# A transformer kernel on Trainium2: masks taken with the maxima on VectorE, weight scaling moved behind the first split, two row transfers in halves, and new orders of work

## The reference, cut to what matters

```
x = layernorm(x + attention0(x))   # 16 heads of width 8, low-rank q and k, causal mask, softmax
x = layernorm(x + ffn0(x))         # silu(x W1) * (x W2), two 512x512 layers with gelu, then W3; each weight has a scale per output
x = layernorm(x + attention1(x))   # 16 heads of width 8, no mask, softmax
x = layernorm(x + ffn1(x))         # one of 8 LoRA experts per token, relu, W_out
```

## Time and profile before

| what | value |
|---|---|
| median of 3 runs | 1014.37 us (1014.31 to 1017.72) |
| the profiled execution's own time | 1017.38 us |
| its span, from the first instruction's start to the last one's end | 1015.4 us |
| PE, DVE, ACT busy | 929.3, 630.3, 469.4 us |
| PE, DVE instructions | 7520, 1643 |
| granted TensorE clock, mean | 0.973 of full speed |

### The profile page before, as it was taken

How to read it: one execution, slowest core, us unless ns; L and a number is a source line. 1 busy time by engine, 2 the same in 40 slices (tenths; PEclk the granted TensorE clock), 3 DMA queues, 4 the chain that set the end, 5 groups by cost and what they waited for, 6 DMA issues and landing times.

```text
span 1015.4 us, 19231 instructions
## 1 busy us (share of the span) xinstructions
PE 929.3 (92%) x7520; PEld 720.2 (71%) x7520; DVE 630.3 (62%) x1643; ACT 469.4 (46%) x935; POOL 164.6 (16%) x261
## 2 busy tenths in 40 slices
PE   4489998999899899988999999999999999999885
PEld 4265875778677678876776887677787867778644
DVE  5555358655965884494588547858666477655643
ACT  0043144653356553345765246556345547363451
POOL 2013023000200420120132014003101013201001
PEclk9997999999999999998999999999999989999888
DMA  8403114202310340240034014301421102011200
GB/s 293 119 8 101 42 53 141 80 3 65 90 53 19 88 117 2 63 132 16 4 101 116 2 49 123 102 5 36 128 72 40 49 23 66 5 36 39 74 3 10
DMA packets 48392, 65.16 MB, mean 64 GB/s; under 512 B 5520, under 2 KB 42640, under 8 KB 43312
## 3 DMA queue, kind: packets, MB, share of 16 engines
q1 hardware_dynamic: 46240, 58.61, 20.4%
q10 hardware_dynamic: 2064, 5.34, 1.4%
HBM read 48.46 MB, written 14.68 MB: 62 GB/s over the span
## 4 chain that ended last, share of the span: by engine, by line
PE 71%; DVE 16%; DMA 6%; issue 3%; ACT 2%; SPq 1%; POOL 1%; ACTq 0%; POOLq 0%; DVEq 0%
PE ps_g L885 21%; PE ps_g L816 10%; PE ps_s L798 8%; PE ps_s L775 7%; DVE top L613 6%; PE ps_g L934 5%; PE ps_g L867 4%; PE ps_s L759 3%; PE ps_g L915 2%; PE ps_g L734 2%; PE ps_g L916 2%; DMA inter<-in_w 2%; DMA krow<-scratch 1%; PE ps_s L767 1%; DMA qrow<-tsplit 1%
## 5 line engine op out<-in xcount | busy, mean ns | idle before, releaser
L613 DVE TENSOR_REDUCE top<-ps_s 128x2 f32<-128x512 f32 (+1 forms) x448 | 288.9, 682 | 161.1 <-PE ps_s L759 87.3
L500 ACT ACTIVATE prob<-ps_s 128x384 f32<-128x384 f32 (+1 forms) x512 | 243.5, 551 | 103.3 <-PE ps_s L798 79.2
L798 PE MATMUL ps_s<-qrow,krow 75*128 75x256 bf16 (+1 forms) x1024 | 151.2, 268 | 8.2 <-DMA qrow<-tsplit 5.0
L775 PE MATMUL ps_s<-krow,qrow 72*128 72x256 bf16 x768 | 148.0, 282 | 8.0 <-DVE top L613 6.7
L816 PE MATMUL ps_g<-prob,v 128*32 128x256 f32 (+1 forms) x2048 | 128.1, 370 | 7.2 <-POOL prob L454 4.9
L522 ACT ACTIVATE hid<-ps_g 128x512 f32<-128x512 f32 x64 | 38.2, 597 | 185.9 <-PE ps_g L885 185.8
L798 PEld LDWEIGHTS ps_s<-qrow,krow 75*128 75x128 bf16 x1024 | 87.6, 100 | 47.9 <-ACT prob L500 23.6
L885 PE MATMUL ps_g<-glu,wh 128*128 128x256 f32 x512 | 120.2, 389 | 0.3 <-DVE glu L683 0.2
L885 PE MATMUL ps_g<-hid,wh 128*128 128x256 f32 x512 | 116.4, 381 | 0.0
L885 PEld LDWEIGHTS ps_g<-glu,wh 128*128 128x128 f32 x512 | 97.5, 195 | 14.8 <-DVE glu L683 0.9
L775 PEld LDWEIGHTS ps_s<-krow,qrow 72*128 72x128 bf16 x768 | 69.6, 100 | 48.8 <-DVE top L613 28.8
(11 more groups left out here) (92 smaller groups left out, 1133.0 us busy)
## 6 DMA issues: line engine op xcount, KB each, us to landing
qrow<-scratch SPq DMA_DIRECT2D x32, 576.0 KB
krow<-scratch SPq DMA_DIRECT2D x96, 192.0 KB
scratch<-split SPq DMA_DIRECT2D x96, 128.0 KB, 1.8
xt<-in_xt SPq DMA_DIRECT2D x16, 128.0 KB, 4.2
x<-in_x SPq DMA_DIRECT2D x16, 128.0 KB, 6.6
wh<-in_wh ACTq DMA_DIRECT2D x1, 2048.0 KB, 14.9
out<-xout SPq DMA_DIRECT2D x16, 128.0 KB, 3.1
qrow<-tsplit SPq DMA_DIRECT2D x96, 8.0 KB, 1.8
```

The source lines that it names most:

```text
L500: nc.scalar.activation(prob[s][:, j % 2, g, 0:wide], ps_s2[:, (GROUP * j + g) % PSUM2, 0:wide], ACT.Exp, scale=1.0 / float(np.sqrt(np.floa ...
L613: nc.vector.tensor_reduce(out=dst, in_=src, axis=AX, op=ALU.max, negate=True).then_inc(maxed[s], 1)
L775: done = nc.tensor.matmul(at, queries(h, qb), keys(h, 2), start=True, stop=s == A1, skip_group_check=True)
L798: done = nc.tensor.matmul(bank[:, kb * SEQ:(kb + 1) * SEQ - q0], krow[s][n % DEEP[s]][0:ROWSM, h, kb * P:(kb + 1) * P], qrow[s][n % DEEP[s ...
```

## The change

- **Masks.** PE's mask matmuls stay for chunks 0 and 1 of A0 (`BY_PE = 2`). From chunk 2 on PE writes bare scores, and DVE replaces the one reduction of a bank by `tensor_tensor_reduce`: (scores + triangle) * -1, written back to PSUM, with the running minimum as the accumulator output. There are four instructions over 128 elements for u = 0 and two over 256 elements for u = 1 and 2. The tile `above` gets a left half of zeros for this.
- **Start.** The scaling of F0's weights becomes a step of DVE's order (`scale`), which stands behind `split_` and `v_` of chunk 0. The first low-rank factor comes in two DMAs, behind the small second one, and PE folds the first half of the pairs while the second may still be on its way.
- **Halved rows.** The fetch of A0's chunk 0 and of A1's chunk 15 is issued as two sets of four DMAs, with heads 0 to 7 first, and pass 1 starts on the first set.
- **Orders.** All strings are new. In PE's, from chunk 2 on, A0's pass-1 banks stood singly 53 times, in pairs 54 times, and once each in a run of three and of four; now they stand singly 107 times, in pairs 25 times, and once each in a run of three and of eight. A1's banks stood singly 90 times and in pairs 83 times; now 144 times singly, 49 times in pairs, three times in threes and once in a five. SP's string begins `oooapap` before (three loads, then park, fetch, park, fetch) and `oaopapdo` after (one load, park, load, fetch, park, fetch, maxima rows, load). DVE's begins `abaccc` before and `abuaccc` after, where u is `scale`. The letters from m to Q are renamed.

```diff
+BY_PE = 2
+HALVED = {A0: 0, A1: CHUNKS - 1}
...
-BARE = ('load', 'resid', 'fetch', 'pass1', 'pass2', 'norm', 'store')
+BARE = ('load', 'scale', 'resid', 'fetch', 'pass1', 'pass2', 'norm', 'store')
...
 SEQUENCE = {
...
     "sp": (
-        "oooapapddapoapodvIdvIaopaypoydvIvIayopPydvIdapPoaypoPdvIvIaPpoPyydvIdapoaypoPddvIvIaPpoyaPpydodvaIpoapyv"
-        "IPydvIydvIPyPvIvIPyPPyPP"
+        "oaopapdodapoapdodapwJoawJzpzdwJdowJzoapQazpdowJdQwJoazpazpdQowJdwJQzaopzapdQowJdwJazopzoQQapdwJwdJQzaopa"
+        "zpQdwJdwJzzQwJwQJzQQzQQQ"
...
+        above = sb("above", [P, 2 * P], BF16)
-        above = sb("above", [P, P], BF16)
...
+        weights0b = sem("weights0b")
...
+        half_spread = per_stage("half_spread")
...
         def _(sp):
-            sp.dma_start(wqa, d_in["qk_a"]).then_inc(weights0, DMA)
+            for half, there in enumerate((weights0, weights0b)):
+                pairs = bass.ts(half, HEADS // 4)
+                sp.dma_start(wqa[:, pairs], d_in["qk_a"][:, pairs]).then_inc(there, DMA)
             def load(s, n):
...
                     sp.wait_ge(spread[s][n % 2], NSPREAD * (n // 2))
+                if n - 2 == HALVED[s]:
+                    sp.wait_ge(half_spread[s], NSPREAD)
...
-                sp.dma_start(qrow[s][n % DEEP[s]][0:ROWS].rearrange("r h t -> r (h t)"),
-                             scratch[s][n % 2][0].rearrange("i (c h) t -> (i c) (h t)", c=HD).unsqueeze(1).to_broadcast(
-                                 [PARTS * HD, PARTS, HEADS * TOK])).then_inc(spread[s][n % 2], DMA)
-                for i in range(PARTS):
-                    sp.dma_start(krow[s][n % DEEP[s]][i * HD * PARTS:(i + 1) * HD * PARTS].rearrange("r h t -> r (h t)"),
-                                 scratch[s][n % 2][1].rearrange("j (c h) t -> c j (h t)", c=HD)).then_inc(spread[s][n % 2], DMA)
+                pieces = 2 if n == HALVED[s] else 1
+                for piece in range(pieces):
+                    heads = bass.ts(piece, HEADS // pieces)
+                    there = spread[s][n % 2] if piece == pieces - 1 else half_spread[s]
+                    sp.dma_start(qrow[s][n % DEEP[s]][0:ROWS, heads].rearrange("r h t -> r (h t)"),
+                                 scratch[s][n % 2][0].rearrange("i (c h) t -> (i c) h t", c=HD)[:, heads].rearrange(
+                                     "r h t -> r (h t)").unsqueeze(1).to_broadcast(
+                                     [PARTS * HD, PARTS, HEADS // pieces * TOK])).then_inc(there, DMA)
+                    for i in range(PARTS):
+                        sp.dma_start(krow[s][n % DEEP[s]][i * HD * PARTS:(i + 1) * HD * PARTS, heads].rearrange("r h t -> r (h t)"),
+                                     scratch[s][n % 2][1].rearrange("j (c h) t -> c j h t", c=HD)[:, :, heads].rearrange(
+                                         "c j h t -> c j (h t)")).then_inc(there, DMA)
             def maxima(s, n, g):
...
-            nc.gpsimd.affine_select(out=above[:], in_=above[:], compare_op=ALU.is_ge, fill=MASKED,
+            nc.gpsimd.affine_select(out=above[:, P:], in_=above[:, P:], compare_op=ALU.is_ge, fill=MASKED,
...
             dve.wait_ge(folded, 1)
-            dve.wait_ge(weights1, NWEIGHTS1)
-            dve.wait_ge(weights2, NWEIGHTS2)
...
+            def scale(s, n):
+                dve.wait_ge(weights1, NWEIGHTS1)
+                dve.wait_ge(weights2, NWEIGHTS2)
+                nc.vector.tensor_tensor(w12[:, 0, :], w12[:, 0, :], scales[:, 0, :], ALU.mult).then_inc(scaled_w, 1)
+                nc.vector.scalar_tensor_tensor(out=w12[:, 1, :], in0=w12[:, 1, :], scalar=0.5, in1=scales[:, 1, :],
...
             def split_(s, n, g):
...
-                if s == A0 and u == 0:
-                    dst, src = top[s][:, 0, h:h + 4], bank.rearrange("p (h k) -> p h k", h=4)
-                else:
-                    qb, pair = (1, u - 1) if s == A0 else (u % 2, u // 2)
-                    dst = top[s][:, qb, h + 2 * pair:h + 2 * pair + 2]
-                    src = bank.rearrange("p (h k) -> p h k", h=2)
+                if s == A0 and n >= BY_PE:
+                    qb, heads, wide = (0, 4, P) if u == 0 else (1, 2, SEQ)
+                    for g in range(heads):
+                        at = h + g if u == 0 else h + 2 * (u - 1) + g
+                        done = nc.vector.tensor_tensor_reduce(out=bank[:, g * wide:(g + 1) * wide], in0=bank[:, g * wide:(g + 1) * wide],
+                                                              in1=above[:, 2 * P - wide:], scale=-1.0, scalar=3.0e38,
+                                                              op0=ALU.add, op1=ALU.min, accum_out=top[s][:, qb, at:at + 1])
+                    done.then_inc(maxed[s], 1)
+                    return
+                heads = 4 if s == A0 and u == 0 else 2
+                qb, pair = (u % 2, u // 2) if s == A1 else (0, 0) if u == 0 else (1, u - 1)
+                dst = top[s][:, qb, h + heads * pair:h + heads * pair + heads]
+                src = bank.rearrange("p (h k) -> p h k", h=heads)
             def maxima(s, n, g):
...
-            walk(dict(qk=split_, v=v_, pass1=pass1, maxima=maxima, outputs=outputs, project=project, down=sum_,
+            walk(dict(scale=scale, qk=split_, v=v_, pass1=pass1, maxima=maxima, outputs=outputs, project=project, down=sum_,
         def _(pe):
-            for side in range(2):
-                for pair in range(HEADS // 2):
+            for pair in range(HEADS // 2):
+                if pair == HEADS // 4:
+                    pe.wait_ge(weights0b, DMA)
+                for side in range(2):
...
             def pass1(s, n, j, u):
-                if j == 0 and u == 0:
+                if j == 0 and u == 0 and n == HALVED[s]:
+                    pe.wait_ge(half_spread[s], NSPREAD)
+                if j == (HALVES if n == HALVED[s] else 0) and u == 0:
                 def keys(h, blocks):
...
                 def mask(at):
-                    return nc.tensor.matmul(at, identb[:], above[:], start=False, stop=True, skip_group_check=True)
+                    return nc.tensor.matmul(at, identb[:], above[:, P:], start=False, stop=True, skip_group_check=True)
+                masked = s == A0 and n < BY_PE
                 if s == A0 and u == 0:
                     for g in range(GROUP):
-                        nc.tensor.matmul(at, queries(GROUP * j + g, 0), keys(GROUP * j + g, 1), start=True, stop=False,
-                                         skip_group_check=True)
-                        done = mask(at)
+                        done = nc.tensor.matmul(at, queries(GROUP * j + g, 0), keys(GROUP * j + g, 1), start=True, stop=not masked,
+                                                skip_group_check=True)
+                        if masked:
+                            done = mask(at)
-                        done = nc.tensor.matmul(at, queries(h, qb), keys(h, 2), start=True, stop=s == A1,
+                        done = nc.tensor.matmul(at, queries(h, qb), keys(h, 2), start=True, stop=not masked,
-                        if s == A0:
+                        if masked:
...
```

More of the change, by code:

```diff
@@ L70 @@
     "i": ("project", A0), "j": ("turn", A0), "k": ("norm", A0), "l": ("osum", A0),
-    "m": ("resid", A0), "n": ("causal", A0), "o": ("load", A0), "p": ("fetch", A0),
+    "m": ("causal", A0), "n": ("resid", A0), "o": ("load", A0), "p": ("fetch", A0),
     "q": ("gated", F0), "r": ("hidden", F0), "s": ("down", F0), "t": ("turn", F0),
[L73 to L78, removed]
+    "u": ("scale", F0), "v": ("norm", F0), "w": ("qk", A1), "x": ("v", A1),
+    "y": ("pass1", A1), "z": ("maxima", A1), "A": ("pass2", A1), "B": ("values", A1),
+    "C": ("outputs", A1), "D": ("merge", A1), "E": ("project", A1), "F": ("turn", A1),
+    "G": ("norm", A1), "H": ("osum", A1), "I": ("resid", A1), "J": ("fetch", A1),
+    "K": ("route", F1), "L": ("lora", F1), "M": ("expert", F1), "N": ("down", F1),
+    "O": ("norm", F1), "P": ("resid", F1), "Q": ("store", F1),
 }
@@ L89 @@
[L89 to L93, removed]
@@ new lines @@
+        "cEcqkccGcccOdcccccqccCccEqccqcsvwxdsyyyyyyvyNyyGbwgyyOyyyaKyybgziyyKyyykiNyykqyyayOyyqyyyyczcxCccccEGccq"
+        "ccqccdccCcccscvcEccwccxcKsdvyyyyywbgyyayyyyyiyyyyNzybGykyyygyyyyyyKyOyyayyqzcccxCicckNcEcOGcqcccCKcqdccc"
+        "cEcqscvcccwcxsvccdwyyNyGyyOyybyygyyayKyyyyzyyiyyyyyyybykyNyyOyyyaxzcCgcEccGqcicccqcckcCccdcccEccqccscqvc"
+        "wcKxcdbyysyyvgyyyiyykyywyyyNyGyOzgqiyyqyKykyyyyyyyxyyCyEyyzNGsqvKqwyyxyOCyyysEyvyNyyGwyyOKyyNyyOzyyyyyyy"
+        "yyyyNyOyyyyzCxEGKCNEGKONO"
@@ L551, in _ @@
             nc.vector.tensor_copy(wq[A0][:].rearrange("p a c -> p (a c)"), ps_g[:, 0, 0:2 * D]).then_inc(wready, 1)
[L553 to L563 removed]
             dve.wait_ge(made, 2)
             last = Last()
+            def scale(s, n):
[3 more added lines that the diff above has]
+                nc.vector.scalar_tensor_tensor(out=w12[:, 1, :], in0=w12[:, 1, :], scalar=0.5, in1=scales[:, 1, :],
```

(7 more changed lines are left out.)

65 lines of the change are left out of this document (28 added, 37 removed).

## The result

The changed kernel takes 966.95 us (median of 4, 964.86 to 979.18) against 1014.5 us for the kernel before on the same chip: ratio 0.955, 95% interval 0.947 to 0.963. Six later runs gave 966.83 us, ratio 0.950 (0.947 to 0.953).

A forecast was written before the change was run, and what follows sets the result against it. PE was taken to bound the body, DVE second, with transfers and DVE's scaling bounding the start. Terms -26 + 8 - 8 - 2 = -28 gave 989.4 us against 1017.38, forecast as a 987 us median; range 970 to 1008, 8 in 10.

The forecast's parts named there:

- What bounds the kernel: Body at PE's pace with DVE a near second; start set by transfers and DVE's scaling.
- Masks off PE, -26.0: Chunks 2 to 15: PE loses 448 mask matmuls at 0.058 us each, gaining at most 26.0 us.
- Masks onto DVE: A0's pass-1 banks, chunks 2 to 15: steps of 0.33 and 0.48 us, 81 us more DVE time in all.
- the low end: Lower bound on DVE's mask price, from steps of 0.205 and 0.38 us in similar rows: 30 us over 14 chunks.
- Body: -26 + 8 = -18 us: Chunks 2 to 15: PE's mask saving of 26 us, less 8 of DVE's 81 us exposed to PE.
- all of the masks' time is kept and the new orders also close some: Rival for the body: full mask saving plus 3 us of PE's 33 us idle; -39 us, median 975, chance 0.2.
- The start, -8: Start: earlier first fetch and chunk 1 rows bring pass 1 forward; -8 us, ends 0 and -12.
- the end, -2: Last A1 fetch: halving lets PE start up to 3 us earlier; -2 us, ends 0 and -4.
- The 1.4 us of the fold: Start: PE's fold begins at 6.0 instead of 7.44 us, as the small factor lands first; 0 to 2.4 us.
- The slower rival: A0's pass 1, chunks 2 to 15: DVE's banks set the pace, 81 us exposed; +45, median 1059, chance 0.1.
- The 44%: Exposed share of DVE's extra 81 us, 36 / 81, above which the change would make the kernel slower.
- PE's waits for DVE's maxima: Sign: these waits rise from 11 to about 20 us; a rise of over 26 us would refute the prediction.

The follow-up runs named there:

- e2: Kernel before with the new orders alone; masks on PE, old start and end: 1000.3 us, ratio 0.984.
- e5: Changed kernel with the old start and end (scaling before the first split, factor and rows in whole pieces): 974.7 us, ratio 0.961.
- e1: Changed kernel with all masks back on PE (`BY_PE = 16`): 990.0 us, ratio 0.975.
- e11: Changed kernel with no causal triangle in pass 1 from chunk 2 on, so no masks on PE or DVE: 969.6 us, ratio 0.954.
- e13: Changed kernel with one more 512-element DVE reduction and a wait ahead of each four-head bank's masks, 56 more: 984.6 us, ratio 0.970.
- e4: Kernel before with the new start and halved rows alone; old orders otherwise, masks on PE: 1008.7 us, ratio 0.994.
- e6: Changed kernel without halved rows at either end; scaling stays behind the split: 972.3 us, ratio 0.959.
- e3: Kernel before with the masks moved to DVE from chunk 2 on, under old orders and old start: 1027.1 us, ratio 1.011.
- e12: Kernel before with DVE's masks from chunk 2 on, old orders and start, but 36 A0 bank pairs parted in PE's string alone: 1037.8 us, ratio 1.022.
- e14: Changed kernel with one more 512-element DVE reduction and a wait ahead of all twelve masked banks, 168 more: 1042.2 us, ratio 1.027.
- e8: Changed kernel with DVE adding the masks of chunks 0 and 1 too (`BY_PE = 0`): 967.3 us, ratio 0.953.
- e15: Changed kernel with A1's and F1's weights loaded after chunk 1's rows, and chunk 1's x before chunk 0's parks: 966.6 us, ratio 0.952.
- e17: Changed kernel with late A1 and F1 weights, chunk 1's x before chunk 0's parks, and DVE's masks in chunks 0 and 1: 965.0 us, ratio 0.950.

## Why the prediction was wrong, step by step

- **What bounds the kernel** held: PE's pace in the body, DVE second. It was told from idle time of 33 us in the body, but that idle time was then only given to a rival with 3 us in it.
- **Masks off PE, -26.0: right in size under the new orders.** e2 to e5 gives -25.6 with DVE's share inside, e1 to e11 -20.4 without it; that the second is the smaller shows the scatter. Under the old orders only 9 to 10 of it arrives. The per-mask price read between neighbours' starts was sound; whether it reaches the end is a property of the order.
- **Masks onto DVE, "81 us in all": the size failed.** 42.3 us of busy time (40 by the steps), near the low end of 30. The step is what counts, and I took 0.33 and 0.48 us, which is the low end's 0.205 and 0.38 with 0.10 to 0.13 more for the accumulator. It measured 0.25 and 0.38: the accumulator adds 0.04 us and nothing. That 0.33 and 0.48 are near the durations (324 and 452 ns) is no merit of the estimate, as the earlier trace rows had shown durations to exceed steps by 0.08 to 0.10 us. The Trainium skill, "VectorE: DVE Perf Modes", section "Two Vector instructions with no wait between them", holds here: 448 operations with an accumulator output left 448 reads of 140 ns. The section "The DRAIN you can't avoid" has the next operation wait until the pipe is empty, but also says that one which is not held starts earlier, which the prediction left out. The timeline shows the second: the next one starts 0.25 us into an operation of 0.33 us, as in the reductions.
- **"Body: -26 + 8 = -18 us": the failed step.** The 8 came out at about 0 (e11 against the changed kernel), and at +15 for a price close to the one I had assumed (e13). The body's real value, -26 - 14 = -40, misses a term that stood in no sum of the forecast: the orders by themselves. I took them as what keeps DVE's new load covered, at nothing of their own, and gave "also close some of the 33 us" a chance of 0.2 and 3 us. e2 shows 14. The rival *all of the masks' time is kept and the new orders also close some* is thus the case that came, at 975 too small by 8. Of the 20 us between forecast and result, 14 are this term and 8 the exposed part of DVE's work; the start and the end give 2 back.
- **The start, -8, and the end, -2: right as a sum** (e5: -8; e4: -7). Bank 0 at 30.1 and bank 1 at 44.3 stand against 29 and 43 predicted, the first fetch at 23.6 against 22.5. The 1.4 us of the fold was nil: the first half of the large factor landed no earlier. The split is only read from traces: about 3 us for the halving at the end (e6), where 2 had been put. But the gap in the earlier trace rows was no ground for it: before 955.22 PE has no idle time in the kernel before, so it wasn't waiting for these rows. Only under the new orders does PE wait there, for 3.0 us in e6.
- **The slower rival** named a mechanism that is real, in the wrong kernel: with the old orders 22 of DVE's 40 us are exposed, and the kernel does get slower (e3). The 44% named as the point from which it decides doesn't carry over, as it divides 36 us by 81: here 22 us stand against the 9 to 10 that taking the masks off PE brings. The pairs of banks were part of my reason for the orders; e12 shows that they are not the whole of it, since parting them on PE alone made it worse.
- **PE's waits for DVE's maxima** were to rise from 11 to 20 us. They fell to 9.2 (3.9 + 3.4 + 1.9) at the same places, a sign that the orders had done more than cover the load.

Open is *which* of the moves in the orders gives the 14 us. In the body 5 us of PE's waits for DVE, 3 for ACT and 3 for POOL are gone (before to e2), so no single place holds them. ACT's higher busy time, 434 us where it was 398, is no sign that pass 2 runs earlier: 24 us of the 36 are the additional table loads. The strings of the engines depend on each other (where one engine puts a step ahead of another's, both can wait for ever), and single strings of old and new were not mixed, so the cause inside the orders is argued, not shown.

## What to carry to other kernels

Where a change brings new orders together with moved work, give the orders a term of their own and bound it by the idle time that the bounding engine has in the body; here it was the second largest term, and the moved work was worth -26 with it and +13 without it. Price a run of like instructions by the step between their starts, not by their durations. Work given to the second engine was free here up to a point and then cost nearly its full time (37, 70 and 144 us cost -3, 15 and 73), so ask how near that point is, and not for one exposed share. And look at what an engine's busy time is made of before reading it as progress: here 24 us of ACT's were table loads.

## What the runs showed of the hardware that was not expected

- An accumulator read is 140 ns long but starts with the next operation. Two statistics over 128 elements step by 0.205 us, the masked maximum by 0.25.
- A table load of ACT takes 1.28 us. The strings' changes between exponential and gelu count 54 of them before and 70 with the new orders, 69 and 90 us.
- A lower mean of the granted clock need not cost time. In e3's profile it was 0.937, with 131 us of records at the lower level, 1.2 GHz, against 0.973 and 57 us in the kernel before. But 44 us of these lie in one stretch at the start, where PE gets as far at either level. From 30 to 60 us, before and then e3:
```profile
30.00:60.00 30.00, 18.55 (x123) 13.08 (x124) 16.86 (x27) 2.43 (x5) 0.00 (x0) 1.00 0.33 93
30.00:60.00 30.00, 18.30 (x122) 12.83 (x122) 16.87 (x27) 2.19 (x5) 0.00 (x0) 0.50 0.33 93
```
  Such a stretch takes some 0.02 off the mean, which would account for runs of the kernel before that took the same time, 1013 to 1019 us, at 0.950 to 0.958 and at 0.973 to 0.980. Outside it e3 has 87 us at the lower level, e12 86 and e14 89, with 50, 56 and 65 us of idle PE in the body; the kernel before has 57 with 33. What these 30 us more cost is open; an estimate from the two levels is at most half, 15 us, so a part of e3's loss may be the clock's.
- The first loads land with a scatter of over 2 us from run to run: PE's projection of chunk 0 began at 15.45 us in the changed kernel's profile, at 17.81 in e8's:
```profile
17.81 2.05 PE L760 MATMUL ps_g<-xt,wq 128*128 128x256 f32 x4 [2.64 <-DMA x<-in_x]
```
  That is as much as e15 to e17 could gain there. The scatter of the first bank is less, 29.1 to 31.0 us in the seven profiles that share the changed kernel's start with halved rows, so the earlier banks of e15 and e17 are real; only the end doesn't show them.
